# Softmax attention stage: sums packed into 32 rows for the reciprocal and spread by transfers, maxima turned in float16, query projection first in a period

## The reference

```python
def _L0_attn_ref(x, Wq, Wk, Wv, Wo, bo):     # x: [8, 512, 128], 16 heads of 64
    q, k, v = (split_heads(x @ W.T) for W in (Wq, Wk, Wv))
    sim = jnp.einsum('bhid,bhjd->bhij', q, k) * DIM_HEAD ** (-0.5)
    e = jnp.exp(sim - max(sim))
    attn = e / (sum(e) + 1e-10)
    out = jnp.einsum('bhij,bhjd->bhid', attn, v)
    return merge_heads(out) @ Wo.T + bo
```

## Time and profile before

| what | value |
|---|---|
| median of 3 runs | 2275.11 us (2273.93 to 2275.41) |
| the profiled execution | 2278.47 us, its span 2276.7 us |
| mean granted TensorE clock | 0.931 |
| busy over the span | PE 1866.1 us (82%), DVE 1669.5 (73%), ACT 1066.1 (47%), POOL 1080.2 (47%) |
| attention, 64 pairs | 268.3 us (first scores) to 1131 us (last maxima) |

### The profile page before, as it was taken

How to read it: one execution, slowest core, us unless ns; L and a number is a source line. 1 busy time by engine, 2 the same in 40 slices (tenths; PEclk the granted TensorE clock), 3 DMA queues, 4 the chain that set the end, 5 groups by cost and what they waited for, 6 DMA issues and landing times. The chain is left out here.

```text
span 2276.7 us, 36764 instructions
## 1 busy us (share of the span) xinstructions
PE 1866.1 (82%) x12205; PEld 1097.1 (48%) x12205; DVE 1669.5 (73%) x3322; ACT 1066.1 (47%) x2294; POOL 1080.2 (47%) x1304
## 2 busy tenths in 40 slices
PE   0555489999999999999935548999948888789999
PEld 0334234444444444444414435666637677656665
DVE  5887677888788877888778875666667777746665
ACT  0112255555555555555511135555537667445555
POOL 0111255555555555555611134555545556345555
PEclk9888599999999999999968977999979999879999
DMA  6000122222222222222100000000000000000000
GB/s 181 0 0 1 28 56 63 61 59 56 60 60 61 57 57 62 60 61 57 43 0 1 0 1 1 1 0 0 0 0 1 1 1 1 1 1 9 9 9 9
DMA packets 77058, 64.53 MB, mean 28 GB/s; under 512 B 12224, under 2 KB 75904, under 8 KB 76928
## 3 DMA queue, kind: packets, MB, share of 16 engines
q1 hardware_dynamic: 71392, 57.41, 9.9%
q10 hardware_dynamic: 5536, 5.52, 0.8%
HBM read 10.32 MB, written 2.10 MB: 5 GB/s over the span
## 5 line engine op out<-in xcount | busy, mean ns | idle before, releaser
L795 ACT ACTIVATE at_pT<-at_turned 128x512 f32<-128x512 f32 x512 | 305.6, 597 | 292.2 <-PE at_turned L862 273.3
L1022 POOL TENSOR_TENSOR m_g<-m_gT,m_g 128x512 f16<-128x512 f32 x260 | 301.4, 1159 | 232.1 <-ACT m_g L1005 232.1
L1036 PE MATMUL m_h<-m_xT,m_w 128*128 (+1 forms) x1572 | 386.8, 383 | 19.9 <-PEq L463 19.9
L694 DVE TENSOR_REDUCE at_nmax<-at_score 128x1 f32<-128x512 f32 x512 | 337.2, 680 | 71.8 <-PE at_score L839 68.7
L673 POOL TENSOR_TENSOR m_w_attn<-at_pT 128x512 f32<-128x512 f32 x128 | 162.4, 1269 | 377.1 <-ACT at_pT L795 377.1
L972 DVE TENSOR_TENSOR m_gT<-m_silu,m_h 128x512 f32<-128x512 f32 x262 | 180.3, 688 | 200.5 <-ACT m_silu L1001 200.4
L1001 ACT ACTIVATE m_silu<-m_h 128x512 f32<-128x512 f32 x262 | 156.6, 598 | 227.1 <-PE m_h L1036 227.1
L716 DVE RECIPROCAL m_w_attn<-m_w_attn 128x512 f32<-128x512 f32 x64 | 214.6, 3353 | 38.6 <-ACT m_w_attn L801 38.6
L900 PE MATMUL at_pv<-at_pT,at_v 128*64 128x512 f32 x1024 | 231.4, 594 | 0.0
L1055 PEld LDWEIGHTS m_y<-m_w,m_g 128*128 128x128 f16 x3072 | 192.9, 98 | 60.5
L1036 PEld LDWEIGHTS m_h<-m_xT,m_w 128*128 128x128 f16 x1572 | 144.3, 99 | 149.6 <-issue 28.3
(11 more groups left out here) (231 smaller groups left out, 3262.6 us busy)
## 6 DMA issues: line engine op xcount, KB each, us to landing
at_both<-at_part_q SPq DMA_DIRECT2D x128, 128.0 KB, 2.4
at_kh<-at_part_k SPq DMA_DIRECT2D x256, 64.0 KB, 2.0
at_both<-at_part_q SPq DMA_DIRECT2D x128, 64.0 KB, 2.0
at_kl<-at_part_k SPq DMA_DIRECT2D x128, 64.0 KB, 2.0
m_x<-in_x SPq DMA_DIRECT2D x8, 256.0 KB, 4.7
at_both<-at_mrow SPq DMA_DIRECT2D x128, 1.0 KB
out_x<-m_x SPq DMA_DIRECT2D x8, 256.0 KB, 2.3
m_wqkv<-in_w_qkv ACTq DMA_DIRECT2D x1, 1152.0 KB, 6.6
```

Source lines behind the costliest of these rows:

```text
L694: nc.vector.tensor_reduce(nmax[head][:, qt:qt + 1], score[use % 2][:], AX.X, ALU.max, negate=True)\
L795: nc.scalar.activation(pT[g % 2][:, head, kt, :], turned[i % 2][:], ACT.Exp).then_inc(exp_done, 1)
L1022: nc.gpsimd.tensor_tensor(g16[u % 4][:, 1, :], gT[u % 4][:], g16[u % 4][:, 0, :], ALU.subtract).then_inc(low_done, 1)
L1036: last = nc.tensor.matmul(bank[:], mem["w12_16"][:, w_part, e, first:first + P], mem["xT"][:, x_part, ds(b * SEQ, SEQ)], start=(i == 0), s ...
```

## The change

The attention stage alone is edited. (1) After `total_out` SP packs one row of sums per head into 16 partitions of 32 (`pack_total`, 2 DMAs), DVE inverts this 32x32 tile, SP writes it to DRAM (`unpack_inverse`, 1 DMA), and reads it back with a broadcast to the 64 partitions of each head (`spread_inverse`, 2 DMAs). (2) `nmax` and the identity are float16, the turn is a plain matmul into the `sums` bank instead of a float32 transpose into a score bank, and the score banks simply alternate. (3) The scales of queries and keys are changed so that the maximum goes unscaled into its row, and the exponential takes a scale of 64. (4) The query projection comes directly after unit 0, the key projection after unit 3 and before the output; the turn of head 0 comes behind the values; the lists of ACT, DVE and SP are rearranged to it. `normalise` moves a period later and `oT` has one buffer.

```diff
-        M_UNIT = 64.0
+        SHRINK = 64.0
+        SCALES = (DH ** -0.5 / W_ATTN / 4.0, 1.0 / W_ATTN / 16.0)
...
+        PACK = 32
+        packed, inv = (s.sb(n, [2 * SEQ // PACK, PACK]) for n in ("packed", "inv"))
+        inv_row = [nc.dram_tensor(f"{tag}_inv_row{i}", [2, SEQ], F32, kind="Internal").ap() for i in range(2)]
...
# SP
                 def max_row(g, head):
-                    sp.wait_ge(s_read, turn_use(g, head) + 1)
+                    sp.wait_ge(m_out, 2 * g + head + 1)
...
+                def pack_total(g):
+                    sp.wait_ge(total_done, g + 1)
+                    for h in range(2):
+                        sp.dma_start(packed[packs[h], :], total[h * DH:h * DH + 1, :].rearrange("o (a b) -> o a b", b=PACK))\
+                          .then_inc(packed_in, 16)
+                def unpack_inverse(g):
+                    sp.wait_ge(rinv_done, g + 1)
+                    if g >= 2:
+                        sp.wait_ge(rinv_in, 32 * (g - 1))
+                    sp.dma_start(inv_row[g % 2].rearrange("h (a b) -> (h a) b", b=PACK), inv[:]).then_inc(inv_row_in, 16)
+                def spread_inverse(g):
+                    sp.wait_ge(inv_row_in, 16 * (g + 1))
+                    if g:
+                        sp.wait_ge(o_done, g)
+                    for h in range(2):
+                        sp.dma_start(rinv[halves[h], :], inv_row[g % 2][h:h + 1, :].to_broadcast([DH, SEQ])).then_inc(rinv_in, 16)
...
                 for g in PERIODS:
-                    if live(g):
-                        max_row(g, 1)
                     if live(g + 2):
...
                         to_rows(g + 2, 0, 0)
+                    if live(g):
+                        max_row(g, 1)
+                    if live(g + 2):
                         sp.wait_ge(lo_done, 2 * (g + 2) + 1)
                         to_rows(g + 2, 0, 1)
-                    if live(g + 1):
-                        max_row(g + 1, 0)
-                    if live(g + 2):
                         sp.wait_ge(hi_done, 2 * (g + 2) + 2)
                         to_rows(g + 2, 1, 0)
                         sp.wait_ge(lo_done, 2 * (g + 2) + 2)
                         to_rows(g + 2, 1, 1)
+                    if live(g - 1):
+                        pack_total(g - 1)
+                        unpack_inverse(g - 1)
+                    if live(g + 1):
+                        max_row(g + 1, 0)
+                    if live(g - 1):
+                        spread_inverse(g - 1)
...
# DVE
+                    nc.vector.tensor_copy(mrow[head][:], sums[0:TPB, 0:P]).then_inc(m_out, 1)
...
                 def inv_total(g):
-                    dve.wait_ge(total_done, g + 1)
-                    nc.vector.reciprocal(rinv, total).then_inc(rinv_done, 1)
+                    dve.wait_ge(packed_in, 32 * (g + 1))
+                    if g:
+                        dve.wait_ge(inv_row_in, 16 * g)
+                    nc.vector.reciprocal(inv[:], packed[:]).then_inc(rinv_done, 1)
                 def normalise(g):
                     dve.wait_ge(pv_done, g + 1)
-                    dve.wait_ge(rinv_done, g + 1)
+                    dve.wait_ge(rinv_in, 32 * (g + 1))
...
                 for g in PERIODS:
                     if live(g + 1):
                         neg_max(g + 1, 0)
                         neg_max(g + 1, 1)
+                    if live(g + 2):
+                        low(g + 2, 0)
                     if live(g):
                         max_row(g, 1)
                     if live(g + 1):
                         neg_max(g + 1, 2)
+                    if live(g - 2):
+                        normalise(g - 2)
+                    if live(g + 1):
                         neg_max(g + 1, 3)
-                    if live(g + 2):
-                        low(g + 2, 0)
-                    if live(g + 1):
-                        max_row(g + 1, 0)
                     if live(g + 2):
                         low(g + 2, 1)
                     if live(g - 1):
                         inv_total(g - 1)
                     if live(g + 1):
-                        neg_max(g + 1, 4)
-                        neg_max(g + 1, 5)
-                    if live(g - 1):
-                        normalise(g - 1)
-                    if live(g + 1):
-                        neg_max(g + 1, 6)
-                        neg_max(g + 1, 7)
+                        max_row(g + 1, 0)
+                        for i in range(4, 8):
+                            neg_max(g + 1, i)
...
# ACT
                     if live(g):
                         exp(g, 0)
-                        exp(g, 1)
-                        exp(g, 2)
                     if live(g + 2):
                         high(g + 2, 0)
                     if live(g):
+                        exp(g, 1)
+                        exp(g, 2)
                         exp(g, 3)
...
# PE
-                    nc.tensor.transpose(score[use % 2][:, 0:P], nmax[head][:], mem["ident"][:]).then_inc(s_done, 1)
+                    nc.tensor.matmul(sums[:, 0:P], nmax[head][:], ident16[:], start=True, stop=True).then_inc(m_done, 1)
...
+                        if i == 0 and live(g + 2):
+                            project(g + 2, 0)
                         if i == 1 and live(g):
                             max_turned(g, 1)
-                        if i == 2 and live(g + 2):
-                            project(g + 2, 0)
                         if i == 3:
+                            if live(g + 2):
+                                project(g + 2, 1)
                             if live(g - 2):
                                 output(g - 2)
-                            if live(g + 2):
-                                project(g + 2, 1)
+                            if live(g - 1):
+                                values(g - 1)
                             if live(g + 1):
                                 max_turned(g + 1, 0)
-                            if live(g - 1):
-                                values(g - 1)
```

More of the change, by code:

```diff
@@ L586, in attn_stage @@
         total, rinv = mem["w_attn"][:, 2, 0:SEQ], mem["w_attn"][:, 2, SEQ:2 * SEQ]
-        nmax = [s.sb(f"nmax{i}", [P, P]) for i in range(2)]
+        nmax = [s.sb(f"nmax{i}", [P, P], F16) for i in range(2)]
+        ident16 = s.sb("ident16", [P, P], F16)
         mrow = [s.sb(f"mrow{i}", [TPB, P], F16) for i in range(2)]
-        oT = [s.sb(f"oT{i}", [P, SEQ]) for i in range(2)]
+        oT = s.sb("oT", [P, SEQ])
         ones = s.sb("ones", [P, DH])
+        PACK = 32
+        packed, inv = (s.sb(n, [2 * SEQ // PACK, PACK]) for n in ("packed", "inv"))
+        inv_row = [nc.dram_tensor(f"{tag}_inv_row{i}", [2, SEQ], F32, kind="Internal").ap() for i in range(2)]
         score = [s.bank(f"score{i}") for i in range(2)]
@@ L604, in attn_stage @@
         PERIODS = range(-2, PAIRS_ALL + 2)
[L606 to L617, removed]
+        M_ALL = 2 * PAIRS_ALL
         with nc.Block() as block:
@@ L691, in neg_max @@
                     head, qt = divmod(i, TPB)
-                    use = score_use(g, i)
-                    dve.wait_ge(s_done, use + 1)
-                    nc.vector.tensor_reduce(nmax[head][:, qt:qt + 1], score[use % 2][:], AX.X, ALU.max, negate=True)\
+                    dve.wait_ge(s_done, UPP * g + i + 1)
+                    nc.vector.tensor_reduce(nmax[head][:, qt:qt + 1], score[i % 2][:], AX.X, ALU.max, negate=True)\
                       .then_inc(s_read, 1)
                 def max_row(g, head):
-                    use = turn_use(g, head)
-                    dve.wait_ge(s_done, use + 1)
+                    dve.wait_ge(m_done, 2 * g + head + 1)
                     if g:
                         dve.wait_ge(m_in[head], 16 * g)
-                    nc.vector.tensor_scalar(mrow[head][:], score[use % 2][0:TPB, 0:P], 1.0 / M_UNIT, None, ALU.mult)\
-                      .then_inc(s_read, 1)
+                    nc.vector.tensor_copy(mrow[head][:], sums[0:TPB, 0:P]).then_inc(m_out, 1)
                 def low(g, which):
                     dve.wait_ge(hi_done, 2 * g + 1 + which)
-                    scale = (DH ** -0.5 / W_ATTN, 1.0 / W_ATTN)[which]
+                    scale = SCALES[which]
                     pair = part[which]
@@ L733, in _ @@
                 nc.vector.memset(nmax[0][:], 0.0)
-                nc.vector.memset(nmax[1][:], 0.0).then_inc(set_up, 1)
+                nc.vector.memset(nmax[1][:], 0.0)
+                nc.vector.tensor_copy(ident16[:], mem["ident"][:]).then_inc(set_up, 1)
                 for i in range(RING):
@@ L740, in _ @@
                 for i in range(RING):
-                    last = nc.vector.memset(kl[i][DH:DH + 1, :, :], M_UNIT)
+                    last = nc.vector.memset(kl[i][DH:DH + 1, :, :], 1.0)
                 last.then_inc(set_up, 1)
@@ L794, in exp @@
                         act.wait_ge(added, 2 * (g - 1))
```

(21 more changed lines are left out.)

20 lines of the change are left out of this document (10 added, 10 removed).

## The result

The changed kernel takes 2378.94 us (median of 4, 2377.17 to 2389.53) against 2274.52 us of the kernel before (median of 4): ratio 1.047, 95% interval 1.0439 to 1.0502. It is slower, and the forecast of 2382 us was 3 us off. The profiled execution took 2379.23 us with a span of 2377.4 us.

What follows compares the result with a forecast made beforehand. PE was taken to bound the kernel at 13.46 us a period; waiting for the pack makes it 15.2, +1.74 us 61 times, +106 us, the ends cancelling: median 2382 us, range 2350 to 2445 us.

Steps and rivals of the forecast that it cites:

- The sum: Attention period counted from its first score through SP, pack, reciprocal and unit 6: 15.2 us, 1.74 more, 61 times, +106 us.
- The eleven issues: SP's transfers ahead of the pack, back to back: 7.02 us, 0.64 each, so the first pack starts at 9.2.
- the 64 KB rows: Nearest transfers with a landing time: 1.9 to 3.5 us, median 2.0; 2.0 was taken for the pack.
- The two terms for the ends of the stage: Once only in attention: three uncovered transfers at the end, +5 us; earlier query projection at the start, some 5 us less.
- each turn goes from float32 at 0.20 us: On PE, to a float16 matmul of 128 columns at 0.05 us; 0.30 us saved a period.
- The bank wait: PE's first turn waits for DVE to free a score bank; the change removes this 0.32 us a period.
- the wait for the low queries: PE's wait within the output, 0.23 us a period, to be covered by the earlier query projection.
- the wait before the output: PE waits 0.6 us for normalise, which DVE reaches late, done at 4.5 us into the period.
- the wait for the pack: DVE's reciprocal waits for it ahead of maxima 4; PE waits 1.95 us before unit 6, absorbing the 0.85 us saved.
- The clock: Rival: the new PE wait lowers the clock, 1.65 us a fall; every second period 2432 us, every period 2482; chance 0.26.
- Late landings: Rival: small transfers land later than 2.0 us; at 2.3 us 2400 us, at 3.0 us 2477 us; chance 0.08.
- Faster after all: Rival: the pack lands before DVE needs it, PE's stream sets a 13.2 us period, -16 us, 2259 us; chance 0.05.

Runs made afterwards that it cites:

- experiment 3: The changed kernel with the packing undone: DVE inverts the whole 128x512 tile at the same place, the five transfers gone; 2257.2 us, ratio 0.992.
- experiment 5: The kernel of experiment 3 with normalise directly behind the low queries on DVE, before max row 1 and maxima 2; 2226.7 us, ratio 0.9795.
- experiment 7: The kernel of experiment 3 with maxima and identity back in float32, turned by a float32 transpose still in the sums bank; 2262.2 us, ratio 0.9952.
- experiment 4: The changed kernel with the query projection back behind unit 2 on PE, its high and low parts back on ACT and DVE; 2519.9 us (one run).
- experiment 8: The changed kernel with pack before low keys, max row 0 before the write, packed reciprocal behind maxima 4, output behind the sums; 2262.8 us, ratio 0.9913.

## Why the prediction was right

**The sum, step by step.** SP starts 2.16 us into the period (703.37 to 705.53; 720.58 from 718.42), as counted. The eleven issues take 7.13 us (720.58 to 727.71), 7.02 were counted. The pack's second transfer lands after 1.7 us, not 2.0, which is also below the lower end of 1.9 that the prediction took from the 64 KB rows. The reciprocal is 0.34 us (0.35). From its start to unit 6 it is 1.14 us (715.30 to 716.44), counted 1.3: the max row behind the reciprocal costs 0.15 us, not 0.28. Unit 6 to the next period 1.98 us (1.97). That gives a period of 14.80 us, not 15.2, and 14.80 is what the undisturbed periods have.

**What cancelled.** The mean is 15.22, and 60 x 0.42 = 25 us above the undisturbed period come from parts that the sum did not have: SP's issues are now and then late (17 us in the stage), and on a loop that runs through SP that is paid; the three falls of the clock are 5 us, and the first full period, with a fourth fall in it, is 3.4 us. The first of these can be read period by period: where the issues of a period are 0.60, 0.94 and 1.06 us late in sum, the period is 0.60, 0.94 and 1.06 us longer. Experiments 3 and 5 have as many late issue rows (23 and 28) and not one of their 60 periods moved: there SP has slack. On the other side the mean before was 13.51, not 13.46: every eighth period is 13.95 us there, with the addition of the residual in it, and the changed kernel has that under its wait. So it was 60 x 1.70 us in place of 61 x 1.74. The two terms for the ends of the stage did not come as sized: -5 us were forecast for the start and -0.9 measured, +5 for the end and -0.6 measured; "they cancel" held for their sum alone. So the mechanism was right, but that the forecast came within 3 us is partly luck: a period 0.4 us too long stood in for late issues and falls of the clock that it did not have. The forecast was closer than its steps.

**PE's own stream.** The turn was mis-sized: "each turn goes from float32 at 0.20 us" took the 0.20 us between the second turn and the sums for its price; experiment 7 shows 0.11 and 0.16, so both together save some 0.15 us, not 0.30. The bank wait and the wait for the low queries did go, and the wait before the output came, 0.5 us for 0.6 forecast. All this made no difference under the wait for the pack, as the prediction said. With the packing undone it shows in part: 7.5 us in the periods of experiment 3, whose period still waits for DVE's reciprocal (0.1 us before unit 6) and for normalise (0.49 us).

**Rivals.** The clock: the mechanism is there, and its price of 1.65 us is right to 0.02 us, but it comes in 4 of the 60 full periods of the changed kernel, with no wait under 2.0 us, and in half of those of experiment 4, whose waits are 2.3 to 3.7 us. The Trainium skill, "TensorE: Matmul & The Clock Gate", section "HAM oscillation — how this bites in real kernels", describes a loop in which a DMA wait made every round start cold. The waits it gives are longer than nearly all of those here, and with these the clock fell in some rounds and not in every one; the measurement decides. Late landings: the pack lands in 1.7 to 1.8 us each time. The read back takes 2.9 us, 0.5 more than the page's other 128 KB transfer (2.4), and no full period waits for it; normalise does so three times, 10.3 us in all, behind 1210 us, at the end of the stage. Faster after all: with the packing kept, only with the lists changed (experiment 8).

## What to carry to other kernels

Count what stands in the queue ahead of a new transfer, and what stands in the engine's list behind the instruction that waits for it. Here an instruction ten times shorter made the kernel 4.7% slower, because 1.7 us of landing and 7 us of issues came before it and the next maxima behind it; the long one had been hidden under matmuls all the time. And ask what a saving on an engine is worth where it isn't the bound: moving one instruction in DVE's list (experiment 5) brought 30 us, while the 3 us saved on each reciprocal brought nothing in the changed kernel; in experiment 5 the wide reciprocal still holds PE up by only 0.1 us a period.

## What was not expected of the hardware

A DMA issue on SP, 0.6 us as a rule, is at times much longer, in all kernels and for most kinds of transfer (never for the 1 KB max row, 128 issues in each of the ten traces). The rows of the low keys, before and in the changed kernel (ns min, median, max):

```profile
L637 SPq DMA_DIRECT2D at_kl<-at_part_k x128: 472/596/1552, 266.9 to 1117.3; - x128
```

```profile
L633 SPq DMA_DIRECT2D at_kl<-at_part_k x128: 472/596/2071, 267.9 to 1212.4; - x128
```

What makes them late was not settled. Before, and with the wide reciprocal, the issues had slack; in a loop through SP they cost some 0.3 us a period, and a range for such a loop should hold them.

A write of 4 KB from SBUF to DRAM lands in 1.3 us (median of 64), sooner than any transfer into SBUF here, and its issue takes 0.31 us, half of the others'.
